# Row-maximum products on 64 by 64 quarters of TensorE, two sets at a time, and roots by one power operation, in an attention and expert kernel

## The reference

```python
x = x + layernorm(attention(layernorm(x)))        # 16 heads of 8, relative positions clipped to +-128
x = x + layernorm(ffn(layernorm(x)))              # 16 experts, top 1, and a shared expert

# attention, with rpk = rel_k[clip(k - q)], rpv = rel_v[clip(k - q)]
scores = (einsum('bhqd,bhkd->bhqk', q, k) + einsum('bhqd,qkd->bhqk', q, rpk)) / sqrt(8)
w = softmax(scores)
out = einsum('bhqk,bhkd->bhqd', w, v) + einsum('bhqk,qkd->bhqd', w, rpv)
```

## Time and profile before

| what | value |
| --- | --- |
| median of 3 runs | 1659.48 us |
| the profiled execution | 1658.59 us |
| its span (first to last instruction) | 1656.9 us |
| TensorE matmul busy | 1527.6 us, 92% |
| TensorE weight load busy | 1180.5 us, 71% |
| VectorE busy | 1237.2 us, 75% |
| ScalarE busy | 1113.8 us, 67% |
| GpSimd busy | 533.5 us, 32% |
| DMA engines, mean busy share | 52% (44.6 + 7.3% for the two program queues) |

### The profile page before, as it was taken

One profiled execution on the slowest core, in us unless ns is written; L12 is line 12 of the kernel. 1 busy time (PEld: TensorE's weight loads), 2 busy tenths in 40 slices (PEclk: granted clock), 3 DMA queues, 4 the chain that ended last, 5 costly groups with the idle time before them and its releaser, 6 DMA issues.

```text
span 1656.9 us, 68421 instructions
## 1 busy us (share of the span) xinstructions
PE 1527.6 (92%) x28642; PEld 1180.5 (71%) x28642; DVE 1237.2 (75%) x3549; ACT 1113.8 (67%) x2053; POOL 533.5 (32%) x1090
## 2 busy tenths in 40 slices
PE   5889899999999999999999999999999997999993
PEld 2347777777777777777777777777777775558992
DVE  7996568787878787878787878787778333753996
ACT  4437677777777777677767776777765775336881
POOL 5523021332232223332323223322202012465567
PEclk9899999999999999999999999999999998999996
DMA  3478855775564456445644564456434672425561
GB/s 84 140 188 217 189 150 113 185 169 140 112 149 103 116 110 148 97 113 117 152 93 113 122 151 91 115 122 145 87 63 92 131 200 48 132 95 152 153 173 51
DMA packets 489140, 212.13 MB, mean 128 GB/s; under 512 B 330663, under 2 KB 462436, under 8 KB 488832
## 3 DMA queue, kind: packets, MB, share of 16 engines
q1 hardware_dynamic: 474112, 165.74, 44.6%
q0 software_dynamic: 14720, 42.03, 7.3%
HBM read 105.73 MB, written 102.85 MB: 126 GB/s over the span
## 4 chain that ended last, share of the span: by engine, by line
PE 64%; DVE 22%; issue 5%; POOL 3%; SPq 3%; DMA 1%; ACT 1%; ACTq 0%; POOLq 0%; DVEq 0%
PE pv L867 11%; DVE mx L1381 11%; PE mix L822 10%; PE sc L845 8%; PE sc L847 6%; PE rel L874 6%; PE mix L824 6%; PE sc L839 3%; PE sc L1029 2%; DVE oS L1409 1%; POOL out_dram L1973 1%; PE sc L965 1%; PE pv L966 1%; PE rel L975 1%; PE mix L884 1%
## 5 line engine op out<-in xcount | busy, mean ns | idle before, releaser
L1121 ACT ACTIVATE w<-sc,escale 128x512 f32<-128x512 f32 x1024 | 686.9, 688 | 339.4 <-PE sc L847 181.6
L1381 DVE TENSOR_REDUCE mx<-mix 128x1 f32<-128x512 f32 x960 | 642.7, 683 | 201.4 <-PE mix L824 190.7
L822 PE MATMUL mix<-WE 128*32 128x512 f16 (+1 forms) x1968 | 389.0, 397 | 42.4 <-DVE mx L1381 31.8
L867 PE MATMUL pv<-w,shared_part 128*9 128x128 f32 x8192 | 371.2, 274 | 1.3 <-issue 1.2
L824 PE MATMUL mix<-Wn,WE 128*32 128x384 f16 (+3 forms) x1968 | 296.1, 305 | 2.8 <-issue 2.8
L845 PEld LDWEIGHTS sc<-shared_part,Wt 96*128 96x128 f16 x5120 | 223.1, 97 | 83.0 <-issue 30.3
L845 PE MATMUL sc<-shared_part,Wt 96*128 96x64 f16 x5120 | 258.4, 192 | 3.1 <-DVE mx L1381 1.8
L874 PE MATMUL rel<-w,shared_part 128*32 128x128 f32 x5120 | 257.8, 273 | 1.4 <-issue 1.4
L867 PEld LDWEIGHTS pv<-w,shared_part 128*9 128x9 f32 x8192 | 203.8, 91 | 75.9 <-issue 44.4
L847 PE MATMUL sc<-shared_part 104*128 104x128 f16 x2560 | 248.3, 218 | 0.0
L1106 ACT ACTIVATE WE<-qp,hmask 128x256 f16<-128x256 f16 x500 | 215.6, 499 | 24.8 <-PE sc L824 24.8
(11 more groups left out here) (263 smaller groups left out, 1999.7 us busy)
## 6 DMA issues: line engine op xcount, KB each, us to landing
qm_d<-ks POOLq DMA_DIRECT2D x48, 512.0 KB, 4.6
shared_part<-qm_d SPq DMA_DIRECT2D x32, 768.0 KB
kt_d<-ks SPq DMA_DIRECT2D x48, 256.0 KB
shared_part<-kt_d SPq DMA_DIRECT2D x128, 96.0 KB
xs_d<-zrow SPq DMA_DIRECT2D x5, 2056.0 KB
vs_d<-vst SPq DMA_DIRECT2D x16, 576.0 KB
shared_part<-vs_d SPq DMA_DIRECT2D x32, 288.0 KB
orl_d<-rel_s SPq DMA_DIRECT2D x512, 8.0 KB
```

The lines of the kernel that those rows point to most:

```text
L822: nc.tensor.matmul(nat[rows, :], lq[:, rows], kn[b2][:, KEYS_AT[t]:KEYS_AT[t] + S], start=True, stop=False, skip_group_check=True)
L867: mm = nc.tensor.matmul(pv[b2][32 * g:32 * g + 9, P * hh:P * hh + P], VC[j][:, b2, 0 if near else 1, h, :], wt[:, :, b2, h, :], start=(j = ...
L1121: nc.scalar.activation(weights, products, ACT.Exp, scale=escale[:, 0:1]).then_inc(s["exp_done"], 1)
L1381: nc.vector.tensor_reduce(mx[:, k:k + 1], nat[:], AX.X, ALU.max).then_inc(s["mx_done"], 1)
```

## The change

Each set of rough scores is now made of products on quarters of the array, 64 rows by 64 columns. The 64 rows are 8 heads of 8 numbers, so a stationary operand holds 8 heads by 8 queries. One call of `natural` makes two sets: the row halves `r` of the array write to two banks (`nats[r]`, heads 0 to 7 and 8 to 15), the column halves `side` to the two halves of a bank's partitions (8 queries each). It is called after every second slot. The sets and the other shared jobs rotate over three banks, `mix[0]` to `mix[2]`; the bank comes from `pv`, whose two sequences now share one bank (9 rows each, 18 in all: the values are stored with nine zeros ahead of them, `VW = 18`, so that the first sequence's product writes both parts). The copy out of `pv` is one per 32 slots, not two. `Qb` and `Qn` halve, and `by_head` takes 8 copies, not 16. Roots are one power operation on GpSimd, `(var + eps) ** -0.5`, in place of the three guess steps (one addition is left on VectorE) and the twelve refining steps; the last two of the run do all 15 steps on VectorE.

```diff
-    Qb = [we16[:, n16 * r:n16 * (r + 1)].rearrange("p (e h q) -> p e h q", e=NE8, h=H) for r in range(2)]
+    Qb = [we16[:, n16 * r:n16 * (r + 1)].rearrange("p (e h k) -> p e h k", e=NE8, h=H8) for r in range(2)]
...
+QUARTERS = tuple((slice(64 * r, 64 * r + 64), r, side) for side in range(2) for r in range(2))
...
-    mix = [pb(f"mix{r}", [P, S]) for r in range(2)]
-    pv = [pb(f"pv{r}", [P, S]) for r in range(2)]
+    mix = [pb(f"mix{r}", [P, S]) for r in range(3)]
+    pv = pb("pv", [P, S])
...
-        shared.append(("row max", slot))
+        if slot % 2 == 1:
+            shared += [("row max", slot - 1), ("row max", slot)]
...
-        return mix[place[job] % 2]
+        return mix[place[job] % BANKS]
...
-        def natural(n, b2, k, nat, tiled):
+        def natural(n, b2, k, nats):
...
-            parts = COLUMN_TILES if tiled else WHOLE_ARRAY
-            for rows in parts:
-                nc.tensor.matmul(nat[rows, :], lq[:, rows], kn[b2][:, KEYS_AT[t]:KEYS_AT[t] + S], start=True, stop=False, skip_group_check=True)
-            for rows in parts:
-                mm = nc.tensor.matmul(nat[rows, near], le[:, rows], Wn[:, x0:x0 + P * (last - first)], start=False, stop=True, skip_group_check=True)
-            mm.then_inc(s["nat_ps"], 1)
+            for rows, r, side in QUARTERS:
+                lq = Qb[half][rows, :, :, 16 * (t % 2) + 8 * side + m].rearrange("p e h -> p (e h)")
+                nc.tensor.matmul(nats[r][64 * side:64 * side + 64, :], lq, kn[b2][rows, KEYS_AT[t]:KEYS_AT[t] + S], start=True, stop=False, skip_group_check=True)
+            for rows, r, side in QUARTERS:
+                le = Qn[half][rows, :, :, 16 * (t % 2) + 8 * side + m].rearrange("p e h -> p (e h)")
+                x0 = WN_0 - P * t - 64 * side - m + P * first
+                mm = nc.tensor.matmul(nats[r][64 * side:64 * side + 64, near], le, Wn[rows, x0:x0 + P * (last - first)], start=False, stop=True, skip_group_check=True)
+                if side == 1:
+                    mm.then_inc(s["nat_ps"], 1)
...
-                mm = nc.tensor.matmul(pv[b2][32 * g:32 * g + 9, P * hh:P * hh + P], VC[j][:, b2, 0 if near else 1, h, :],
+                mm = nc.tensor.matmul(pv[32 * g:32 * g + 9 + 9 * b2, P * hh:P * hh + P], VC[j][:, b2, 0 if near else 1, h, 9 - 9 * b2:VW],
...
-                if nxt:
-                    wait_for_bank(pe, ("row max", slot), i, prev, nxt, nxt2)
-                    natural(i + 1, slot // 64, slot % 64, bank("row max", slot), abs(slot // 32 - slot // 8 % 4) > 1)
+                if nxt and slot % 2 == 1:
+                    pair = (("row max", slot - 1), ("row max", slot))
+                    for job in pair:
+                        wait_for_bank(pe, job, i, prev, nxt, nxt2)
+                    natural(i + 1, slot // 64, slot % 64 - 1, [bank(*job) for job in pair])
...
             for part in range(2):
-                sp.dma_start(dst[ROWS_TERM + part, t], ms[:, part, 16 * t:16 * t + 16]).then_inc(s["ms_st"], 16)
+                for g in range(2):
+                    sp.dma_start(dst[ROWS_TERM + part, t, g], ms[:, part, 16 * t + 8 * g:16 * t + 8 * g + 8]).then_inc(s["ms_st"], 16)
...
         for e in groups:
-            c = OFF0 - WN_0 - 16 * e
-            eng.dma_start(Wn[HD * e:HD * e + HD, 0:WN_W], rpart[0][:, c:c + WN_W]).then_inc(s[landed], 16)
+            c = OFF0 - WN_0 - 8 * e
+            for r in range(2):
+                eng.dma_start(Wn[64 * r + e:64 * r + 64:NE8, 0:WN_W], rpart[0][:, c:c + WN_W]).then_inc(s[landed], 16)
...
             c = 2 * n + half
-            pool.wait_ge(s["ln_step"], 12 * c + 6 * (k + 1))
-            refine(rstd2, var2, rtmp2, "root2", 2 * c + k)
+            pool.wait_ge(s["ln_step"], 8 * c + 4 * (k + 1))
+            pool.tensor_tensor(rstd2[:], var2[:], power[:], ALU.pow).then_inc(s["root2"], 1)
```

More of the change, by code:

```diff
@@ L43 @@
 H, HD = 16, 8
+H8 = H // 2
 M = 128
@@ L117, in attention, with root_guess_step @@
             attention_phase(nc, ctx, locals())
-def root_guess_step(eng, k, mean_var, half, root):
+def root_guess_step(eng, k, half, root):
     if k == 0:
-        return eng.tensor_scalar(half[:], mean_var[:, :, 1], EPS, 0.5, ALU.add, ALU.mult)
+        return eng.tensor_scalar(half[:], half[:], 0.5, None, ALU.mult)
     if k == 1:
@@ L468, in store_qn @@
             sp.wait_ge(s["qsplit"], 3 * c + 2)
-            sp.dma_start(qn_d[bass.ds(c * P, P)], qp[b2][:].rearrange("p e t b -> p (e t b)")).then_inc(s["qn_st"], 16)
+            rows = qn_d[bass.ds(c * P, P)].rearrange("(h r d) n -> r h d n", r=2, d=HD)
+            for r in range(2):
+                sp.dma_start(rows[r], qp[b2][64 * r:64 * r + 64].rearrange("p e a m -> p (e a m)")).then_inc(s["qn_st"], 16)
         def store_q(n, b2):
@@ L1175, in _ @@
         for step in range(2):
[L1176 to L1177 removed]
+            prep(0, 1, step, pv)
+        by_head(0, 0, 1, range(H8))
         for step in range(2, 7):
[L1179 removed]
+            prep(0, 1, step, pv)
         for half in range(2):
[L1181 removed]
+            by_head(0, 1, half, range(H8))
         for step in range(7):
[L1183 to L1184 removed]
+            prep(1, 0, step, mix[2])
+        by_head(1, 0, 0, range(H8))
         act.wait_ge(s["pe_set"], 3)
@@ L1187, in _ @@
         turns(act, turn)
-        for b2 in range(2):
-            outputs(NP - 1, NT - 1, b2)
+        outputs(NP - 1, NT - 1)
         def silu(u):
@@ L1274, in moments @@
             ins.then_inc(s[step], 1)
-            for k in range(3):
-                dve.wait_ge(s[step], base + 2 + k)
-                root_guess_step(nc.vector, k, mean_var, half, rs).then_inc(s[step], 1)
+            dve.wait_ge(s[step], base + 2)
+            nc.vector.tensor_scalar(half[:], mean_var[:, :, 1], EPS, None, ALU.add).then_inc(s[step], 1)
         def normalize(dst, src, mean_var, rs, root, roots, tiles=range(NT)):
             if tiles[0] == 0:
-                dve.wait_ge(s[root], NEWTON_STEPS * (roots + 1))
+                dve.wait_ge(s[root], roots + 1 + (LAST_ROOT_STEPS - 1) * max(0, roots + 1 - (4 * NP - 2)) * (root == "root2"))
             for t in tiles:
@@ L1302, in prep @@
                     bias = vb[:, v:v + 1, :].rearrange("p o (h d) -> p o h d", d=HD).broadcast_to([P, nt, H, HD])
-                    ins = nc.vector.tensor_tensor(vst[:, tiles, far, :, 0:HD], src[:, tiles], bias, ALU.add)
+                    ins = nc.vector.tensor_tensor(vst[:, tiles, far, :, 9:9 + HD], src[:, tiles], bias, ALU.add)
                 ins.then_inc(s["v_ev"], 1)
```

206 lines of the change are left out of this document (105 added, 101 removed).

## The result

The changed kernel takes **1720.7 us** (median of 4, 1718.5 to 1722.7) beside 1658.4 us for the kernel before on the same chip (median of 4): a ratio of **1.0376, 95% interval 1.0349 to 1.0403**. It is 62 us slower, where a kernel 64 us faster, of 1594 us, was forecast.

A forecast was written before the change was run, and what follows sets the result against it. TensorE was taken as the bound, with VectorE's order of work making the stalls. 1658.6 us less 39 (TensorE's products), less 28 (stalls), plus 2 (prologue) gave 1594 us; own range 1570 to 1615, wider range 1545 to 1645.

The forecast's parts named there:

- the sentence on DMAs: SyncE's queue: four stores of maxima a group for two add 11 us a turn, spread over 165, costing nothing.
- The bound: TensorE sets the pace in the turns with sets: 158 of 165.6 us a turn, the other 7 to 8 stalls.
- TensorE's terms: Sets on TensorE: halved streaming, less 0.10 us per tiling change and 0.10 per pair for loads; 39 us saved in seven turns.
- The saving of 5.5 us a turn: TensorE, sets on quarters: 4.2 us a turn from near slots and 1.3 from far ones.
- the 0.10 put on the loads: TensorE: weight loads of a pair's quarters show as 0.10 us per pair, bounds 0 and 0.22 or more.
- The estimate of 0.05 by the Trainium skill: TensorE: loading 64 columns would show only 0.05 us, making the sum gain 22 us more; not followed.
- Roots: Layernorm roots by one GpSimd power, under 1 us: wait goes, VectorE gains; part of 28 us of stalls saved.
- The third bank: Sets: VectorE may hold three sets through the values, so finishing work no longer stalls TensorE; part of the 28 us.
- the copy out of the one `pv` bank: Copy after each 32 slots: due at the same slot as the earlier second copy, so it costs nothing.
- Prologue: Before the turns: faster sets bring nothing, and later loads of `Wn` and one more store lose 2 us.
- The slower one: TensorE: row halves' loads or streams queue, about 1700 us; sign: under 425 exponentials per 550 us; chance 0.15.
- VectorE taking over: Far stretches run at VectorE's pace, so only work leaving VectorE counts: 34 us saved, 1625 us; chance 0.17.

The follow-up runs named there:

- b_half: The kernel before with roots by one power operation and each maximum over the first 256 keys alone; 0.9598 of the kernel before.
- b_less: The kernel before with roots by one power operation and, in far tiles, without the second product of each set; 0.9724 of the kernel before.
- a_noqn: The changed kernel with two 16-column stores of maxima a group, not four, and no loads of `Qn` after the prologue; 0.9867 of the kernel before.
- b_pow: The kernel before with the roots by one power operation alone; 0.9855 of the kernel before, and 0.9889 when run again.
- a_mm: The changed kernel with maxima stored from ScalarE's queue in the turns and four stores of `pv` for eight; 1.0173 of the kernel before.
- a_mm_half: As a_mm, but each maximum is taken over the first 256 of the 512 keys; 1.0010 of the kernel before.
- b_dma: b_pow with the old products and DMAs made like the change's, with 4 issues a turn more than the change; 1.0158 of the kernel before.
- a_again: The changed kernel itself, run again on another set's chip as reference; 1.0360 of the kernel before.

## Why the prediction was wrong

**The step that failed** is the sentence on DMAs: "store_max issues four instead of two; at 0.67 us an issue the 8 groups of a turn add 11 us to SyncE's queue, spread over 165, and the results are needed some 30 slots, 39 us, later: nothing." It asked when the stored maxima are needed. The cost is in what stands behind them on SyncE's list: `load_o` had 18 us of lead, the next turn's first keys and values 8 slots. The list was full to 0.65 before, which one sum over its issues would have shown. Second, the 11 us were less than a third of what came on it, 38 us a turn: the price was that of a load of `Wn`, while the stores of maxima added 17 us by their durations; the loads of `Qn` kept their number and bytes but reach 16 partitions 8 apart, and one issue went from 0.44 to 0.75 us, 10 us a turn; the rest is longer issues of other kinds. That makes 0.86. Third, the text did say "each late load would cost its lateness once a turn", but gave it no chance, and one late load costs more than its lateness: 5.1 us of stall and then 3 us at half the clock.

**The bound** (TensorE at 158 of 165.6 us, stalls 7.5) was right: with the stalls gone a turn of b_half is 157.6 us, and b_less falls with TensorE's work.

**TensorE's terms** were right nearly to the hundredth. Scores to pair 0.33 (806.62 to 806.95), first product 0.32 (803.45 to 803.77), second with the change back 0.26 (803.77 to 804.03); the four starts of a group lie 3 to 6 ns apart. The saving of 5.5 us a turn shows wherever the DMAs leave it alone: turns 3 to 6 of a_noqn, 159.0 us on average, against 163.9 of b_pow, 4.9 us; turn 6 of a_mm, 156.4, against 161.4 in b_pow. The first product takes 0.32 us where 512 columns stream in 0.22, so the 0.10 put on the loads shows. The estimate of 0.05 by the Trainium skill, TensorE: Matmul & The Clock Gate, section LDWEIGHTS, which the prediction did not follow, was lower than these 0.10. The saving shows in these turns alone; over the whole run a_noqn is no faster than the roots alone, as said above.

**Roots** were right in kind. The power takes 1.02 us where under 1 was taken, the wait of `y` for GpSimd is off the list, and the roots alone are worth 18 to 24 us; the prediction had 28 us for them and the third bank together, which it did not divide.

```profile
L1892 POOL TENSOR_TENSOR rstd<-var,power 128x4 f32<-128x4 f32 x30 | 30.6, 1020 | 240.9 <-DVE var L1290 240.9
```

**The third bank** shows no gain. TensorE's stalls over 0.6 us in turn 3 sum to 7.7 us before, 4.7 in b_pow, and 7.8 in a_noqn: those at slots 69, 80 and 99 (1.2 to 1.4 us) wait for VectorE's finishing and placing steps, the one at 106 (1.6 us) for the copy out of the one `pv` bank, which the prediction costed at nothing. So the bank did not give its part of the 28 us here; three banks with the old products were not tried, so what it does by itself stays open.

**Prologue**: 2 us forecast, 8 measured. The first maximum is at 32.5 us instead of 28.0, and with fewer columns to stream TensorE is granted 0.61 of its clock there (0.90 before). VectorE, which set the pace there, is idle for 10 of 92 us, not 3; that the clock is the reason was not tested.

**The rivals.** The slower one, at about 1700 us, came near 1720.7 by luck: its reason is refuted, since no row halves queue (the starts above). Its sign came true all the same, 410 exponentials in 550 us, under 425, so that sign did not belong to it alone. VectorE taking over is refuted by a_mm_half. Summed up, against the kernel before: roots -18 to -24 us, the array's saving about -34 (7 x 4.9), prologue +8; to come out at +62 the rest must be 106 to 112. Taking stores of maxima and the loads of `Qn` away gives back 4.9%, 82 us: 2 to 3% of it, 34 to 49 us, shown as the late list and what follows it, the rest not divided between list and packets. The other 24 to 30 us are still there in a_noqn: the stalls for `pv` and for the finishing steps, and turns 0 to 2 (168.1, 162.1 and 166.7 us against 159.0 later). That the DMAs cost the old products 3.0% and the new ones 4.9% (where more was taken away) was not taken apart further; a TensorE with less to do stands idle longer at the same lateness, and the means of the clock (0.98 to 1.00 in turns 1 to 6 of b_dma, 0.94 to 0.98 in a_again) fit that, but no run isolates it.

## What to carry to other kernels

Before a DMA is added to an in-order queue, sum the queue's issues over a period and find the load behind it with the least lead; that load, not the result of the one added, is what pays. An issue has a price by its form, so a layout that keeps count and bytes can still fill the queue. And where two changes come as one, run each alone: here the small one won 1.1 to 1.5%, and the large one lost 5%; the roots alone are the version to keep.

## What the runs showed that was not expected

The time of an issue on SyncE depends on form and company: a load of `Qn` took 0.44 us on average for 8 adjacent partitions, 0.60 for 8 that lie 8 apart, 0.75 for 16 that lie 8 apart, and 0.95 to 0.99 in the variants in which ScalarE issued the stores of maxima (0.57 to 0.73 us each there). The medians are 0.33, 0.57, 0.60 and 0.60, so the form shows in the typical issue and the company only in a tail of long ones. Two queues did not issue side by side at full rate. On quarters of TensorE, two row halves and two column halves streamed together without loss, and the exits and entries cost 0.10 us as for 32-wide tiles. The granted clock fell where TensorE had less to do and VectorE set the pace: 0.61 instead of 0.90 in the prologue.
